# Attention with shifted positions: two writes and then two reads on the sync queue, in place of one write and one read in turn

## What is computed

```python
def _relative_shift(x):
    b, h, s, _ = x.shape
    x = jnp.pad(x, ((0, 0), (0, 0), (0, 0), (1, 0)))
    x = x.reshape(b, h, s + 1, s)
    return x[:, :, 1:, :].reshape(b, h, s, s)

content_score = jnp.einsum('bhsp,bhtp->bhst', q + u, k)
pos_score = jnp.einsum('bhsp,htp->bhst', q + v, pos)
pos_score = _relative_shift(pos_score)
score = (content_score + pos_score) / jnp.sqrt(jnp.float32(P))
weights = jax.nn.softmax(score, axis=-1)
out = jnp.einsum('bhst,bhtp->bhsp', weights, val)
```

## Time and profile before

| what | value |
|---|---|
| median of three executions | 5282.39 us |
| the profiled execution | 5275.38 us |
| its span, first to last instruction | 5273.6 us |
| PE busy over the span | 5009.2 us, 95% |
| DVE, ACT, GpSimd busy | 70%, 66%, 27% |
| DMA moved over the span | 1391.53 MB |
| writes of positions (L348) | 512 of 1026.0 KB |
| reads of shifted positions (L356) | 512 of 1024.0 KB |
| clearing of the experts' buffer (L1190) | 8 writes of 2048.0 KB, from 3528.9 us on |

### The profile page before, as it was taken

The page is one execution under the profiler, slowest core; times in us unless marked ns, Lnnn a source line. Parts: engine busy times, 40 slices in busy tenths (PEclk is TensorE's granted clock), DMA queues, the critical chain, the costliest instruction groups (busy, mean ns, idle before and its releaser), DMA issues. The chain is left out here.

```text
span 5273.6 us, 126103 instructions
## 1 busy us (share of the span) xinstructions
PE 5009.2 (95%) x42412; PEld 3733.9 (71%) x42412; DVE 3698.8 (70%) x7976; ACT 3456.6 (66%) x5116; POOL 1435.4 (27%) x1032
## 2 busy tenths in 40 slices
PE   7899999999999999999999999979999999999997
PEld 3566666666666666666666666658888898988987
DVE  7699888787787887887878888864444444433344
ACT  3688787787787887887878888854333333333444
POOL 0111111111121111111211121114555555544443
PEclk9899999999999999999999999989999999999998
DMA  9899999999999999999999999985444455433349
GB/s 359 314 344 339 327 339 332 331 334 331 329 335 332 339 327 336 331 327 329 340 326 336 335 334 340 346 292 146 102 115 121 110 124 131 108 58 64 58 120 316
DMA packets 320387, 1391.53 MB, mean 264 GB/s; under 512 B 42816, under 2 KB 120384, under 8 KB 188352
## 3 DMA queue, kind: packets, MB, share of 16 engines
q1 hardware_dynamic: 270528, 1315.45, 73.4%
q0 software_dynamic: 49152, 67.14, 7.3%
HBM read 708.20 MB, written 674.23 MB: 262 GB/s over the span
## 5 line engine op out<-in xcount | busy, mean ns | idle before, releaser
L677 DVE CUSTOM_DVE_ANT_0 att_shifted<-att_quad,att_shifted 128x512 f32<-128x512 f32 x2048 | 1331.9, 684 | 263.6 <-PE att_quad L921 203.7
L542 ACT ACTIVATE att_shifted<-att_shifted,att_mn 128x512 f32<-128x512 f32 x2048 | 1360.8, 717 | 132.5 <-issue 126.0
L537 ACT ACTIVATE att_xo<-att_quad 128x1024 f32<-128x1024 f32 x1024 | 1048.3, 1024 | 464.8 <-PE att_quad L909 464.3
L687 DVE COPY att_pt<-att_tp 128x512 f32<-128x512 f32 x1536 | 1011.8, 686 | 204.9 <-PE att_tp L942 203.7
L942 PE MATMUL att_tp<-att_ident,att_shifted 128*128 128x128 f32 x8192 | 1147.2, 284 | 1.0 <-ACT att_shifted L542 0.4
L942 PEld LDWEIGHTS att_tp<-att_ident,att_shifted 128*128 128x128 f32 x8192 | 899.2, 143 | 306.2 <-issue 283.4
L1385 DVE TENSOR_TENSOR ffn_hp<-ffn_hf,ffn_hp 128x512 fp32r<-128x512 f32 x512 | 467.4, 913 | 769.4 <-ACT ffn_hf L1335 769.2
L1333 ACT ACTIVATE ffn_hp<-ffn_up 128x512 fp32r<-128x512 f32 x512 | 305.8, 597 | 1021.0 <-PE ffn_up L1462 1020.9
L909 PE MATMUL att_quad<-att_pos,att_qv 64*128 64x512 f32 x2048 | 854.9, 457 | 40.2 <-ACT att_xo L537 40.0
L1423 PE MATMUL ffn_yp<-ffn_w2p,ffn_hp 128*128 128x256 f32 x6144 | 838.3, 287 | 29.1 <-DVE ffn_w2p L1397 19.8
L1423 PEld LDWEIGHTS ffn_yp<-ffn_w2p,ffn_hp 128*128 128x128 f32 x6144 | 809.1, 193 | 68.6 <-issue 29.2
(11 more groups left out here) (108 smaller groups left out, 4812.8 us busy)
## 6 DMA issues: line engine op xcount, KB each, us to landing
xs_d<-att_xo SPq DMA_DIRECT2D x512, 1026.0 KB, 9.7
att_shifted<-xs_d SPq DMA_DIRECT2D x512, 1024.0 KB, 8.7
att_shifted<-in_L_attn_x_dram SPq DMA_DIRECT2D x32, 512.0 KB, 7.2
xn_d<-att_shifted SPq DMA_DIRECT2D x32, 512.0 KB, 6.4
xt_d<-att_shifted SPq DMA_DIRECT2D x32, 512.0 KB, 7.5
att_xf<-xt_d SPq DMA_DIRECT2D x32, 512.0 KB, 9.3
att_d<-att_osb SPq DMA_DIRECT2D x512, 32.0 KB
ffn_d<-ffn_zero SPq DMA_DIRECT2D x8, 2048.0 KB, 24.1
```

The costliest lines, as they stand in the source:

```text
L537: act.activation(xo[:, kk % NW, 2 * half:2 * half + 2, 1:S + 1], xp[:, :, :], ACT.Copy).then_inc(x_out, 1)
L542: act.activation(shifted[:, kk % NX, t], shifted[:, kk % NX, t], ACT.Exp, bias=mn[:, kk % NX, t:t + 1], scale=-1.0).then_inc(exp_done, 1)
L677: dve.tensor_tensor_reduce(out=shifted[:, kk % NX, t], in0=sp_[:, t % 2], in1=shifted[:, kk % NX, t], scale=-0.25, scalar=-NEG, op0=ALU.ad ...
L687: dve.tensor_copy(pt[:, t], tp[:, t % 2]).then_inc(t_out_dve, 1)
```

## The change

The order of SP's writes and reads. At every even head of a pass SP now issues the writes of heads kk + 3 and kk + 4 and then the reads of heads kk + 2 and kk + 3; at odd heads neither. Each write and each read keeps its own waits. The load of a sequence and the small stores stay at their heads, behind the reads. Ahead of the loop there is one write and one read less. Other engines are not changed.

```diff
                 sp.wait_ge(p_low, DC)
                 sp.wait_ge(w_low, 1)
-                for k in range(LEAD - 1):
+                for k in range(LEAD - 2):
                     write_x(0, k)
                     if k == 2:
                         for n in range(NS):
@@ -383,10 +383,14 @@
                     first = isinstance(i, int) and i == 0
                     last = isinstance(i, int) and i == ITERS - 1
                     for kk in range(BH):
-                        if not (last and kk + LEAD - 1 >= BH):
-                            write_x(i, kk + LEAD - 1)
-                        if not (last and kk + LEAD - 2 >= BH):
-                            read_x(i, kk + LEAD - 2)
+                        if kk % 2 == 0 and not (last and kk + LEAD - 2 >= BH):
+                            write_x(i, kk + LEAD - 2)
+                            if not (last and kk + LEAD - 1 >= BH):
+                                write_x(i, kk + LEAD - 1)
+                        if kk % 2 == 0 and not (last and kk + LEAD - 3 >= BH):
+                            read_x(i, kk + LEAD - 3)
+                            if not (last and kk + LEAD - 2 >= BH):
+                                read_x(i, kk + LEAD - 2)
                         if kk % H == 4 and not last:
                             load_xt(i * 2 + 2 + kk // H)
                         if kk % QH == 0 and not (first and kk < 2 * QH):
```

## The result

| | before | after |
|---|---|---|
| median of five timed runs, us | 5282.39 | 5338.23 |
| lowest to highest, us | 5267.68 to 5290.23 | 5312.59 to 5355.27 |
| ratio, 95% interval | 1 | 1.0104 [1.0071, 1.0136] |
| profiled execution, us | 5275.4 | 5339.39 |
| its span, us | 5273.6 | 5337.6 |

The forecast was 5225, with a range up to 5290. The sign was wrong and the time lies outside the range.

What follows compares the result with a forecast made beforehand. PE was taken to set the attention loop's pace, with DMA just slower and stalls at the seams. From 5275.4 us, -27 for turns and -26 for the seam gave 5222, forecast as 5225; range 5165 to 5290.

Steps and rivals of the forecast that it cites:

- What bounds the kernel: Attention loop: PE sets the pace at 6.14 us a head, DMA is just slower at 6.29; seams and late landings lose time.
- (a): Write-to-read turns on the DMA engines, 1.1 to 1.3 us each, halved; need falls to about 5.7 us a head: -27 us.
- (b): Even heads' reads move behind the write two heads on, one head later; 1.8 to 3 us of cover stays.
- first rival: Even heads' reads land too late for their adds: 5317 at 11.5 us latency, 5462 at 12.5; chance 0.12.
- (c): Small stores and batch load behind two reads on SP's queue: at most 1 to 2 us show on a write; 0.
- (d): Seam between passes: SP branches one head earlier, so its stall falls before ACT's; -2 us a seam, -26 us.
- seams under 29: Sign for the seam gain: the three heads between passes take under 29 us, with ACT's gaps summing below 10 us.
- (e): Prologue ahead of the loop: one write less, and R2 issued with the loop's first pair; 0.
- Second rival: Turn costs by bytes, or the dip is not saved: DMA need stays 6.29 us a head, time 5270 to 5290; chance 0.12.
- The sum: Profiled execution: 5275.4 - 27 - 26 = 5222; with the median of runs 7 above the profiled one, forecast 5225.
- share below 0.95: Sign for saved turns: DMA share in 400 to 3400 us falls below 0.95 at about the same GB/s.
- DVE's waits at every second head: Sign of being wrong: in the attention loop, DVE's waits for landings appear at every second head.

Runs made afterwards that it cites:

- b_pool: The kernel before, old order, with the eight small stores issued from GpSimd's queue instead of SP's: 5234.55 us, 0.9972 of before.
- mid_halves: The kernel before, old order, with the small stores between a head's write and its read, split into four at every second head: 5202.31 us, 0.9917.
- late_halves: The kernel before with each read one head later, write and read still in turn, stores on SP split into four every second head: 5200.74 us, 0.9914.
- streams: DMAs alone, computation left out: 48 heads' writes and reads per stretch; without waits 5.20 us a head in turn, 5.46 two and two, 5.56 four and four.
- a_pool: The kernel after, new order, with the eight small stores issued from GpSimd's queue instead of SP's: 5319.54 us, 1.0153 of before.
- a_mid: The kernel after, new order, with the eight small stores issued by SP between the pair's two writes: 5270.82 us, 1.0054 of before.
- b_mid: The kernel before, old order, with the eight small stores issued by SP between a head's write and its read: 5229.87 us, 0.9956.
- b_late: The kernel before with every read one head later, one write and one read still in turn, stores on SP: 5222.39 us, 0.9945.
- b_late_pool: The kernel before with every read one head later, write and read in turn, and the small stores on GpSimd's queue: 5239.96 us, 0.9986.

## Why the prediction was wrong, step by step

**What bounds the kernel** was half right. The missing time of the 29 heads does lie in late landings, and without them PE's pace is what I had read: 178.4 us in b_pool, mid_halves and late_halves against the 178.34 worked out. But the step from a share of 0.98 and 6.29 us a head to "the DMA engines are just slower than PE" failed. Unheld, they do a head in 5.20 us, so they have almost a microsecond a head in hand; late_halves moves the same bytes a head and has two late landings over the loop. What was short was the queue's time on SP, of which I had priced only the stores.

**(a), the turns, failed at its root.** Forecast: 1.1 to 1.3 us for each turn, half of them saved, need 5.7 us, term -27. I had read the dip correctly and given it to the wrong cause. Where writes turned to reads in the loop of before, they also waited: odd heads' reads go out a median of 0.19 us after their write's landing, even heads' 0.56. The one group meant to separate the two, shows a dip of that size in another stage, and I didn't look at what else was moving there: GpSimd issues an indirect store at 3574.33 us, and behind the one at 3568.69, where the clearing just goes on and nothing turns, the slices of 1 us fall to 342 and 327 GB/s as well. In streams a turn costs nothing, and groups of two cost 0.26 us a head. In after, the packets' own time per head fell from 6.16 to 5.89 us, 0.27 and not the 0.6 forecast, and this time bought nothing, since the engines idled for more than that. Nor is it the saving of turns: in late_halves, with a turn at every head, it is 5.91. A row in which turns occur without the wait would have been needed, and before had none; I should have taken "no gain" for the lower bound at a larger chance than 0.12.

**(b), the moves, failed in the latency.** The dependency was named rightly: even reads hang on the copy two heads on, the bound is 10.7 or 11.9 us, and the latency decides. I took 7.5 us to land, from the shortest of the earlier trace rows (6.9), plus 1 us for the queue. Measured in after: 11.8 in the median, 14.2 at 90%, 109 of 225 above 11.9. The sentence that carried this, on the first rival, was "the first write of the pair is issued 6 us before and is gone by then". A write takes a median of 7 to 8 us to land in after and up to 14.8 (12.1 in the bout above), so after 6 us it is not gone. Worse, the odd read that waits for it holds SP until then, a median of 5.1 us after the next write's issue and 8.4 at 90%, enters late, and stands right ahead of the next even head's transfers. "Nothing else is asked of it" overlooked that the second read of the pair asks for the landing of the pair's first write.

**The first rival** is what happened, in its mechanism and nearly in its condition: it asked for "one more transfer" ahead in the queue, some 3 us more to the landing, and the landings came that late. Its price, 5317 to 5462, holds 5338 near the lower end. By its own sum the measured median of 11.8 us costs 1.1 us at the 52 tight pairs, 57 us, and gives 5332; that this is so close is in part luck, since it gives all pairs one latency and puts the whole loss at the tight ones, while one age in ten is above 14.2 us and 109 of 225 are above 11.9. It had a chance of 0.12, which was too small for a case whose own rows said that reads took up to 12.1 us.

**(c), the stores, was mis-sized**: forecast 1 to 2 us late on one write in four heads, measured 6.0 us in the median (8.1 in the bout above). I had added the 6.3 us of the stores but not the wait of the read ahead of them. Little of it is new, though: in before the same write is 5.2 us behind its copy. And it isn't the cause of the loss, as a_pool shows, though another place for the stores gives back half of it (a_mid), by way of the seam. In the old order the stores' place is worth more than I thought: 0.28% by b_pool, 0.44% by b_mid. Off SP they are not always better: of the late orders the one with the stores on GpSimd is the slower (0.9986 against 0.9945), so issuing them there has a price of its own, which isn't located.

**(d), the seam**, came out at a third of the size: -9 us where -26 was forecast. That is 0.7 us a seam, from one profile of each kernel, while single seams go from 23.2 to 32.5 us before and from 22.1 to 30.8 after, so not even the sign is clear of that spread. Of its signs, "seams under 29" was met (28.85), with the ACT gaps of the earlier trace rows here at 2.51 and 6.32 us, 8.8 in sum where they had been 11.9:

```profile
1430.65 0.72 ACT L546 ACTIVATE att_shifted<-att_shifted,att_mn 128x512 f32<-128x512 f32 x1 [2.51 <-issue]
1437.69 0.72 ACT L546 ACTIVATE att_shifted<-att_shifted,att_mn 128x512 f32<-128x512 f32 x1 [6.32 <-DVE att_mn L681]
```

Whether the data queue has a share in the gaps stays open. The seams move with its order: 24.7 (a_mid), 26.0 (late_halves) and 26.3 us (b_late) where before has 29.5. But they don't follow how free the queue is: 28.0 in b_pool, where no add waits for a landing, and 29.0 in b_late_pool, which has neither stores nor holds on it. What fills them isn't shown; no run changed the loop itself.

**(e)**, the prologue at nothing, stands: the spans differ by what the 13 passes differ.

**Second rival**: it said that the turn isn't saved, which was true, and that the time then stays, which wasn't, for the reason in (b).

**The sum** has a slip of its own: 5222 for the profiled execution and 7 more for the median make 5229, not 5225. It changes nothing here.

Of the signs named ahead, "share below 0.95" came true while the time rose, because I had tied it to "about the same GB/s" and that clause did the work (327 against 334). "DVE's waits at every second head" as the sign of being wrong is word for word what the trace shows.

What stays open: how much of the +73 us is waiting and how much PE at 1.2 GHz behind the waits (276 us at that clock against 191); and what makes a seam 24.7 us long in one kernel and 29 in another, which is most of what b_late and a_mid gain.

## What to carry to other kernels

A queue whose engine waits for a landing before it issues is a serial chain: price each entry by when the wait ahead of it ends, not by the transfer's own latency. Put behind a write first the work that needs nothing (0.9956 in b_mid, 0.9917 in mid_halves), or let a dependent read stand one step further back, if something spaces the writes so that it is then no longer held. Late and unheld was never worse than before (0.9945, 0.9986); late and held was slower in all three kernels that have it (1.0054, 1.0104, 1.0153). Before giving a dip to a cause, find a row in which that cause occurs without the other candidate, and if there is none, measure the pattern with nothing else around it.

## What the runs showed of the hardware that I had not expected

Writes to HBM and reads from it of 1 MB, in turn in a full queue, ran at 412 GB/s (5.20 us a head), faster than writes alone (376) and only just slower than reads alone (422); grouped in twos or fours they fell to 388 and 385. I had taken the mix for the slow case.

A wait for the landing between write and read takes 0.6 us from each head even while other transfers are in flight (365 GB/s, with slices of 295 and 238). Placing the read two writes behind its own does not lift it in a full queue: 5.71 us a head, each read still held.

The page "DMA: Bandwidth & Descriptors" of the Trainium skill, Rules for kernel authors, advises to issue a DMA early and to wait on its semaphore late. For the even reads the case agrees: issued later, their cover was eaten. For a read that must wait for a write's landing the two halves of the advice pull apart, since to issue the read early is to wait for the write early. b_late gives up the first half and keeps the second, and is 0.55% faster than before; with the stores on GpSimd the same move brings nothing (0.9986 against 0.9972). So the runs show that the later wait does no harm, and not that it pays everywhere.

For each of the eight small stores SP is occupied 0.5 to 0.8 us (1.87 and 3.09 us for four), and with the same bytes it matters how they stand in a queue of 1 MB transfers: 6.3 us in one piece or about 3.2 twice makes 0.3% (b_late 0.9945, late_halves 0.9914).
